# Self-attention of a transformer block on one core: eight blocks per stage with two value groups each, a fourth bank for the first pass, and sums inverted in another layout

## The reference

```
xn = layer_norm(x, ln0_w, ln0_b)
q, k, v = split(xn @ qkv_w.T)              # 16 heads of 32 features
attn = softmax(q @ k.T * 32**-0.5)         # per head, 2048 queries x 2048 keys
sa = merge(attn @ v) @ sa_proj_w.T
```

## Time and profile before

| | us |
|---|---|
| three timed runs | 3681.93 median (3677.66 to 3685.92) |
| the profiled execution | 3683.99 |
| its span, first to last instruction | 3682.2 |
| self-attention phase, by the trace | 318 to 2104 |

### The profile page before, as it was taken

How to read it: one execution, slowest core, us unless ns; L and a number is a source line. 1 busy time by engine, 2 the same in 40 slices (tenths; PEclk the granted TensorE clock), 3 DMA queues, 4 the chain that set the end, 5 groups by cost and what they waited for, 6 DMA issues and landing times. The chain is left out here.

```text
span 3682.2 us, 52183 instructions
## 1 busy us (share of the span) xinstructions
PE 3365.0 (91%) x16432; PEld 2104.9 (57%) x16432; DVE 2215.5 (60%) x3731; ACT 1545.2 (42%) x2794; POOL 1701.3 (46%) x507
## 2 busy tenths in 40 slices
PE   7998999999999999999999668898876689999999
PEld 6885544444444444444444156556535568888887
DVE  4445878887888888888888125666644632222222
ACT  3230666666666666666666512442422321111111
POOL 0001788888888888888878622342322200000000
PEclk9997999999999999999999887898957889999999
DMA  4547347465465746546553453333315741111110
GB/s 171 180 163 183 71 100 161 87 133 116 96 131 107 155 86 140 115 97 131 107 118 74 106 146 95 116 112 108 90 53 206 263 163 46 46 46 46 46 46 23
DMA packets 178499, 412.01 MB, mean 112 GB/s; under 512 B 20289, under 2 KB 43399, under 8 KB 158831
## 3 DMA queue, kind: packets, MB, share of 16 engines
q1 hardware_dynamic: 156271, 273.87, 24.4%
q0 software_dynamic: 18432, 134.23, 18.2%
q10 hardware_dynamic: 3584, 1.05, 0.1%
HBM read 146.08 MB, written 102.56 MB: 68 GB/s over the span
## 5 line engine op out<-in xcount | busy, mean ns | idle before, releaser
L1591 DVE TENSOR_REDUCE self_part_max<-self_first 128x1 f32<-128x512 f32 x2048 | 1277.9, 676 | 299.9 <-PE self_first L1448 296.6
L1549 ACT ACTIVATE self_expo<-self_second 128x512 f32<-128x512 f32 x2048 | 1068.0, 603 | 690.0 <-PE self_second L1464 656.4
L1397 POOL TENSOR_TENSOR self_pair_sum<-self_expo 128x2048 f32<-128x2048 f32 x192 | 882.8, 4598 | 117.4 <-ACT self_expo L1549 93.9
L1448 PE MATMUL self_first<-self_k,self_q 96*128 96x512 f32 x2048 | 884.6, 439 | 40.9 <-DVE self_part_max L1591 24.2
L1464 PE MATMUL self_second<-self_q,self_k 98*128 98x512 f32 x2048 | 813.4, 400 | 13.5 <-ACT self_expo L1549 13.4
L1448 PEld LDWEIGHTS self_first<-self_k,self_q 96*128 96x128 f32 x2048 | 394.6, 193 | 559.1 <-DVE self_part_max L1591 445.2
L1477 PE MATMUL self_weighted<-self_expo,self_v_sb 128*32 128x512 f32 x4096 | 546.3, 605 | 9.1 <-ACT self_unscaled L1561 6.9
L1464 PEld LDWEIGHTS self_second<-self_q,self_k 98*128 98x128 f32 x2048 | 388.5, 190 | 109.6 <-ACT self_expo L1549 47.7
L1943 DVE CAST mlp_h_high<-mlp_h 128x512 fp32r<-128x512 f32 x128 | 54.7, 427 | 505.6 <-PE mlp_out_sum L61 504.6
L1918 ACT ACTIVATE mlp_h<-mlp_hidden_sum,mlp_b_col 128x512 f32<-128x512 f32 x128 | 88.0, 688 | 601.1 <-PE mlp_hidden_sum L61 601.1
L1397 POOL TENSOR_TENSOR self_half_sum<-self_expo 128x2048 f32<-128x2048 f32 x64 | 292.7, 4579 | 82.9 <-ACT self_expo L1549 82.9
(11 more groups left out here) (165 smaller groups left out, 4130.7 us busy)
## 6 DMA issues: line engine op xcount, KB each, us to landing
self_half_sum<-self_pair_sum POOLq DMA_DIRECT2D x128, 1024.0 KB, 7.2
self_k<-k_t SPq DMA_DIRECT2D x96, 256.0 KB, 9.7
self_q<-q_t SPq DMA_DIRECT2D x93, 256.0 KB, 4.5
cross_q<-cross_r_high SPq DMA_DIRECT2D x256, 64.0 KB, 2.0
qkv_x<-in_x SPq DMA_DIRECT2D x8, 1024.0 KB, 5.4
v<-qkv_v_sb SPq DMA_DIRECT2D x32, 256.0 KB, 2.0
q_t<-qkv_r_high SPq DMA_DIRECT2D x32, 256.0 KB, 2.0
q_t<-qkv_r_low SPq DMA_DIRECT2D x32, 256.0 KB, 2.3
```

Source lines behind the costliest of these rows:

```text
L1397: nc.gpsimd.tensor_tensor(to, expo[:, t % p_slots], expo[:, (t + 1) % p_slots], ALU.add).then_inc(pair_done, 1)
L1448: nc.tensor.matmul(first[:, in_ring[n]], q[0:base, c % q_slots, a, s * P:(s + 1) * P], k[0:base, c // stages_per_group % 2, a, k0:k0 + TOK ...
L1549: nc.scalar.activation(expo[:, t % p_slots, a], second[:, n % ring], ACT.Exp, scale=scale).then_inc(exp_done, 1)
L1591: nc.vector.tensor_reduce(part_max[:, a * SUB + s, k:k + 1], first[:, in_ring[n]], AX_X, ALU.max).then_inc(first_read, 1)
```

## The change

- The period has 8 blocks of eight steps (`blocks = 8`). Two value groups stand at the end of each.
- `first` has four banks. The transposed maxima and the sums take places in the ring of three banks of `second` (`s_uses`, `s_slot`); there is no bank `total` any more. `turn_after` is 1.
- All three sum groups stand behind the value groups of block 1 of the next stage (`sum_block`). ScalarE copies the sums out of PSUM at once, after the 16th exponential (`take_total`), into `inverse`.
- SP lays the four rows of sums (one per head, 512 numbers) out over 128 partitions x 16 by four transfers (`send_sums`). VectorE inverts that in one instruction in block 3. SP writes it to a DRAM row per head, waits for that, and reads it back spread over the 32 partitions of each head by four transfers (`spread_inverse`). VectorE multiplies in block 5.
- ScalarE copies `weighted` straight into `mean`, after the tenth exponential, once the store before has landed. It sends the maxima after exponential 55 (before: 55 as well, counted over the stage).
- GpSimd's half sums and pair sums share four buffers that change roles from stage to stage (`sum_parts`).

```diff
-    blocks = n_k
-    per_block = heads
+    blocks = 8
+    per_block = n_seconds // blocks
-    turn_after = 2
-    ring = 3
+    turn_after = 1
+    f_ring = 4
+    s_ring = 3
-    sums_at = {15: [(0, 0)], 2: [(-1, 1)], 3: [(-1, 2)]}
-    last_sum, invert_from, max_sent = 3, 5, 13
+    sum_block, take_sum_after = 1, 2 * per_block - 1
+    invert_at, divide_at, max_sent_after = (3, 1), (5, 1), 55
...
+    s_uses = []
+    for j in range(blocks):
+        for at in range(per_block):
+            if first_of[j][at] == (2, turn_after - 1):
+                s_uses.append("turn")
+            s_uses.append(j * per_block + at)
+        if j == sum_block:
+            s_uses.append("total")
...
-        first = m.psum("first", [P, ring, TOK])
-        second = m.psum("second", [P, ring, TOK])
+        first = m.psum("first", [P, f_ring, TOK])
+        second = m.psum("second", [P, s_ring, TOK])
         weighted = m.psum("weighted", [P, TOK])
-        total = m.psum("total", [P, TOK])
+        total = second[:, s_slot["total"]]
+        turned_max = second[0:n_max, s_slot["turn"], 0:P]
...
+                def send_sums(i):
+                    ge(sp, total_read, i + 1, alone=True)
+                    for a in range(heads):
+                        rows = slice(a * HEAD_DIM, (a + 1) * HEAD_DIM)
+                        sp.dma_start(sums[rows], inverse[a * HEAD_DIM:a * HEAD_DIM + 1].rearrange("o (j k) -> o j k", k=share)
+                                     ).then_inc(sums_loaded, 16)
+
+                def spread_inverse(i):
+                    ge(sp, inverse_done, i + 1, alone=True)
+                    sp.dma_start(inverse_rows.rearrange("a (j k) -> (a j) k", k=share), sums[:]).then_inc(inverse_stored, 16)
+                    ge(sp, inverse_stored, 16 * (i + 1), alone=True)
+                    for a in range(heads):
+                        sp.dma_start(inverse[a * HEAD_DIM:(a + 1) * HEAD_DIM],
+                                     inverse_rows[a].unsqueeze(0).to_broadcast([HEAD_DIM, TOK])).then_inc(inverse_loaded, 16)
...
                 def take_weighted(i):
                     ge(act, weighted_done, n_k * (i + 1))
-                    ge(act, mean_done, i)
-                    nc.scalar.activation(unscaled[:], weighted[:], ACT.Copy).then_inc(weighted_read, 1)
+                    ge(act, out_stored, 16 * i)
+                    nc.scalar.activation(mean[:], weighted[:], ACT.Copy).then_inc(weighted_read, 1)
+
+                def take_total(i):
+                    ge(act, total_done, n_sums * (i + 1))
+                    ge(act, mean_done, i)
+                    nc.scalar.activation(inverse[:], total, ACT.Copy).then_inc(total_read, 1)
...
-                def invert(i, part):
-                    if part == 0:
-                        ge(dve, total_done, n_sums * (i + 1))
-                    cols = slice(part * (TOK // pieces), (part + 1) * (TOK // pieces))
-                    nc.vector.reciprocal(total[:, cols], total[:, cols]).then_inc(inverse_done, 1)
+                def invert(i):
+                    ge(dve, sums_loaded, 16 * heads * (i + 1))
+                    nc.vector.reciprocal(sums[:], sums[:]).then_inc(inverse_done, 1)
 
                 def divide(i):
-                    ge(dve, inverse_done, pieces * (i + 1))
+                    ge(dve, inverse_loaded, 16 * heads * (i + 1))
                     ge(dve, weighted_read, i + 1)
-                    ge(dve, out_stored, 16 * i)
-                    nc.vector.tensor_tensor(mean[:], total[:], unscaled[:], ALU.mult).then_inc(mean_done, 1)
+                    nc.vector.tensor_tensor(mean[:], inverse[:], mean[:], ALU.mult).then_inc(mean_done, 1)
```

## The result

| | before | after |
|---|---|---|
| median of the runs, us | 3683.93 (3677.66 to 3689.51, 4 runs) | 3745.48 (3732.51 to 3758.92, 4 runs) |
| span of the profiled execution | 3682.2 | 3742.6 |
| distance between row maxima | 53.6 | 55.3 |

The ratio is 1.0156, 95% interval 1.0125 to 1.0186: slower by 1.6%, where 3592 us and faster was forecast, and outside the range (3569 to 3660).

The account below looks back on a forecast made before the run. TensorE was taken as the bound. Stage: 53.6 - 2.7 - 0.6 - 0.5 + 0.4 = 50.2, written 50.4; 29 stages' 92.8 + 3.7 + 1 - 7.4 = 90.1 us saved, giving 3592 us, range 3569 to 3660.

Parts of the forecast that it names:

- the multiplication: VectorE's multiplication, 0.6 of its cadence, now in a block of eight: costs 0.4 us a stage, bounds -0.5 and 0.
- The third rival: Reads of the inverse land behind the second accumulating transfer; VectorE waits 5.3 us at the multiplication: 3743 us, slower; chance 0.10.
- The plain block: New block with four more pairs and one more value group: 5.77 us against 6.11, gain 2.7 us a stage.
- fourth rival: Two value groups at a block's end do not join: the 2.7 us gain is lost, 3670 us; chance 0.04.
- The transposed maxima: Block where VectorE's split follows one read: excess 0.59 us against 1.16 before, gain 0.6 a stage, bounds 0 and 0.9.
- The send: ScalarE's send of the maxima, now at the end of block 6: gain 0.5 us a stage, bounds 0 and 0.53.
- The copy: ScalarE's `take_weighted` shifts later exponentials: 0.35 us, plus 0.05 for `take_total`, against 0.38 before; net 0, bounds -0.5 and +0.4.
- The second rival: Maxima land late at the next stage's first product, up to 8.7 us: 0 to 1.8 a stage, to 3644; chance 0.12.
- The end of the phase: After the last sums, copy, transfers and inversion take 10.8 us instead of 3.44 of inversions: -7.4 us.
- The first rival: GpSimd becomes the bound through longer accumulating transfers: stage 51.2 to 52.2 us, 3615 to 3644 us; chance 0.15.

Follow-up runs that it names:

- the pair in the kernel before: Kernel before with its multiplication one block later, in block 14: operands as before 3685.58 us, ratio 1.0005; both inputs in SBUF 3777.26 us, ratio 1.0259.
- the first experiment: Changed kernel with VectorE's multiplication in block 5 replaced by a reduction over the spread inverse, one SBUF input: 3622.2 us, ratio 0.982.
- the run with block 7: Changed kernel with VectorE's multiplication in block 7 instead of block 5, some 12 us later: 3746.61 us, ratio 1.015.

## Why the prediction was wrong

**The step that failed** is the multiplication: "-0.4, bounds -0.5 and 0". It was costed by the 0.68 us of the earlier trace rows, in which one input lay in PSUM, and the only question asked was in which block it stands. That its inputs had changed, from `total` in PSUM and `unscaled` in SBUF to `inverse` and `mean`, both in SBUF, stands in the diff and was passed over, and with it what runs on GpSimd at that time. It measured 10.73 - 5.78 = 4.9 us per stage, of which some 3.0 are TensorE's wait, 0.4 the forecast cost of the multiplication itself, and the remaining 1.5 products at the lower clock behind the wait. That last part is a remainder, but the pair in the kernel before puts the price of such a fall at 1.7, with as much clock withheld (0.16 of 10.99 us there, 0.37 of 4.60 here). 50.4 + 4.9 - 0.4 = 54.9, near the 55.3 measured.

The multiplications of the kernel before could not have given a price: 26 of the 32 lie between GpSimd's additions, and the other six have one input in PSUM and take 0.68 to 0.69 us all the same. But another phase of the same trace has the case. In the second `token_phase` VectorE subtracts two tiles in SBUF (L486) while GpSimd does the same to two others (L253):

```profile
2772.91 4.51 POOL L253 TENSOR_TENSOR late_a_low<-late_a_raw,late_a_high 128x2048 fp32r<-128x2048 f32 x1 [9.53 <-ACT late_a_high L378]
2774.59 4.98 DVE L486 TENSOR_TENSOR late_w_low<-late_w_raw,late_w_high 128x2048 fp32r<-128x2048 f32 x1 [15.47 <-ACT late_w_high L384]
2778.54 5.44 POOL L253 TENSOR_TENSOR late_a_low<-late_a_raw,late_a_high 128x2048 fp32r<-128x2048 f32 x1 [1.12 <-ACT late_a_high L378]
...
L486 DVE TENSOR_TENSOR qkv_w_low<-qkv_w_raw,qkv_w_high x3: 2284/2284/2292, 11.4 to 22.2; 128x2048 fp32r<-128x2048 f32 x3
```

The same line takes 2.28 to 2.29 us where nothing of GpSimd runs beside it, and 4.98 here, begun inside GpSimd's instruction. A bound was left out as well: an instruction that waits for GpSimd can cost a whole addition, 4.58 us, and two where they stand without a pause. The Trainium skill (SBUF — State Buffer, Who interferes with whom) states that rule: an instruction of VectorE with two SBUF inputs contends with one of GpSimd that reads SBUF, with at most one SBUF input (outside some faster modes) it does not, and the loser is blocked for the winner's whole instruction. Both halves agree with the pair of runs in the kernel before, 3.24 us against 0.68. The 8.04 us in the run with two inputs in block 13 go beyond it: there the wait took in the next addition too.

**The third rival** named almost the time (3743, a wait of 5.3 us at the multiplication) and the wrong mechanism. Its reads of the inverse were not late in any stage but the last two, where nothing is left to hide them: the 128 landed in 2.0 us at the median, and the run with two blocks more for them was no faster. A forecast that had put its weight there would have been right by chance.

**What held.** The plain block: 5.78 for 5.77, so two value groups join as a value and a sum group do (fourth rival down). The transposed maxima: 0.71 over a plain block, 0.59 forecast. The send: 0. The copy: block 1 was 8.73, with 2.55 for the sums, 0.40 for it, 0.35 forecast. The multiplication with one SBUF input: 6.20 - 5.79 = 0.41, 0.4 forecast. Together 50.4, as the first experiment's regular stage. The second rival, late maxima, did not show: they landed in 5.3 us at the median and 7.4 at most (6.2 and 7.4 in the earlier trace rows). The end of the phase: sums complete at 2155.1, multiplication at 2164.3, so 9.2 us for the 10.8 forecast.

**What would have been missed in any case.** Without the contention the kernel is 0.982 of before, not 0.976: the distances of the first experiment's maxima add up to (50.95 - 50.4) x 31 = 17 us over the regular ones. Its first is 6.8 shorter than a regular one (in the kernel before, 6.4); the five stages with the inversion's wait give 9.1; and two are 57.2 and 57.9 long, 14.3 in all over 50.4, where in the kernel before they were 57.5 and 55.5, 5.8 over 53.6. In these two TensorE stands for 4.5 and 4.6 us (2.3 and 1.8 before) with nothing in the profile that it waits for, behind the 9th and the 17th stage of the second pass, which is where its loop over eight stages begins anew. The forecast worked out the way of the sums for a stage without loads of keys, and let the two stages at the start of the loop gain as the others do. It also stopped its range at 3660, below its own fourth rival (3670); nothing rests on that. The first rival, GpSimd as bound, was 1.2 us away as said, and came true when 1.3 us were added to it.

**Left open**: what TensorE waits for where its loop begins anew, and why that grew from 4.1 us for both places together in the kernel before to 9.1 in the first experiment. And why the clock fell in each of the 30 stages of the changed kernel that have the wait, but only in 16 of 29 in the kernel before with two inputs in SBUF.

## What to carry to other kernels

When a change moves an operand between PSUM and SBUF, the instruction is a different one even if its shape and its time alone stay the same: list for each instruction of VectorE how many inputs lie in SBUF, and for those with two what GpSimd runs beside them. A waiting engine does not always show idle time; a duration whose median is many times its minimum, and whose end keeps a fixed distance from another engine's end, is a wait too. Look for such a pair in the other phases of the same trace: its price may stand there already. The remedy is placement or another engine: between two additions the same instruction cost 0.69 us, on GpSimd itself 1.28.

## What was not expected of the hardware

- The wait stands inside the instruction's record: 3.73 us of duration with no idle time before it, ended 0.55 to 0.56 us after GpSimd's addition in each of the 30 stages. GpSimd's additions were not longer for it (4.55 and 4.56 beside it), since they had begun first. Where VectorE begins first it is GpSimd's record that grows: 4.99 us behind the multiplication at 1021.53 in the run with block 7, and in the kernel before 5.44 where 4.58 is the median of L253.
- The wait can take in two additions: 8.04 us in the run with two inputs in block 13, 7.61 in the one in block 14.
- It costs more than it lasts. 3.0 us of extra duration took 4.5 us from the stage, since the granted clock of TensorE was 0.63 in the 4.6 us after its wait and 1.00 before it. The clock does not fall behind every such wait: it stayed at 1.00 in 13 of 29 stages of the kernel before with two inputs in SBUF.
- Small transfers of 2 KB in pieces of 64 bytes landed in 1.7 us at the median (1.6 least), no slower than the 2.0 taken from the store. (The section that the prediction cites for a fixed cost is on transfers that GpSimd issues; these are SP's.)
